# A GNN encoder's edge sort: bucket matrix with two-byte operands, products moved between engines and steps

## The reference

```python
x = emb[x_ids]
def _spmm(row, col, vals, x):
    msg = vals[:, None] * x[col]
    return jax.ops.segment_sum(msg, row, num_segments=N)
def _layer(x_prev, row, col, vals, W_a, b_a, W_b, b_b):
    h = _spmm(row, col, vals, x_prev)
    z = (h + x_prev) @ W_a.T + b_a + h * x_prev @ W_b.T + b_b
    return jnp.where(z >= 0, z, NEG_SLOPE * z)
# x1 = _layer(x, ...); x2 = _layer(x1, ...); x3 = _layer(x2, ...)
return jnp.concatenate((x, x1, x2, x3), axis=1)
```

## Time and profile before

| what | value |
|---|---|
| median of 3 runs | 9519.62 us (9513.02 to 9523.34) |
| time of the profiled execution | 9515.19 us |
| its span | 9513.4 us |
| busy over the span: PE, DVE, ACT, POOL | 92%, 83%, 46%, 60% |
| first reduce of the first pass | 242.8 us |
| last reduce of the second pass | 3179.3 us |

### The profile page before, as it was taken

How to read it: one execution, slowest core, us unless ns; L and a number is a source line. 1 busy time by engine, 2 the same in 40 slices (tenths; PEclk the granted TensorE clock), 3 DMA queues, 4 the chain that set the end, 5 groups by cost and what they waited for, 6 DMA issues and landing times.

```text
span 9513.4 us, 228026 instructions
## 1 busy us (share of the span) xinstructions
PE 8731.2 (92%) x69832; PEld 8032.5 (84%) x69833; DVE 7879.5 (83%) x11265; ACT 4383.1 (46%) x13668; POOL 5665.0 (60%) x3637
## 2 busy tenths in 40 slices
PE   7688886888888589999999999999999999999999
PEld 4577775577777479999999999999999999999999
DVE  7799998899999788877777788877777788877777
ACT  0578775177777346651111366631111566611112
POOL 8688886088888412228888422258888122278885
PEclk8788888888888689999999999999999999999999
DMA  2211111011111887778888677778889577788886
GB/s 80 37 6 6 6 6 19 7 6 6 6 6 6 27 180 280 280 278 284 287 286 286 196 279 281 280 279 287 286 286 286 192 279 282 281 281 286 287 286 205
DMA packets 1005649, 1718.92 MB, mean 181 GB/s; under 512 B 378356, under 2 KB 429624, under 8 KB 1004920
## 3 DMA queue, kind: packets, MB, share of 16 engines
q0 software_dynamic: 378656, 958.17, 33.8%
q1 hardware_dynamic: 499680, 751.43, 21.8%
q10 hardware_dynamic: 127224, 8.24, 3.0%
HBM read 961.68 MB, written 755.66 MB: 181 GB/s over the span
## 4 chain that ended last, share of the span: by engine, by line
PE 66%; DVE 20%; issue 9%; ACT 2%; DMA 1%; ACTq 1%; DVEq 0%; POOL 0%; SPq 0%; POOLq 0%
PE ps L951 34%; PE ps L942 24%; DVE place L1116 7%; DVE hT L1137 4%; DVE hT L1132 4%; PE ps L789 3%; DVE place L1119 2%; ACT work L713 1%; DVE hT L1260 1%; PE ps L839 1%; PE ps L959 1%; PE ps L979 1%; PE ps L980 1%; PE ps L813 1%; DVE place L1121 0%
## 5 line engine op out<-in xcount | busy, mean ns | idle before, releaser
L951 PE MATMUL ps<-work 128*128 128x125 f32 x28416 | 3281.8, 278 | 37.6 <-DVE work L1313 37.6
L951 PEld LDWEIGHTS ps<-work 128*128 128x128 f32 x28416 | 3240.6, 192 | 78.9 <-DVE work L1313 38.8
L547 POOL DMA_INDIRECT work<-messages,work x1776 | 2709.2, 1525 | 621.7 <-issue 621.7
L942 PE MATMUL ps<-xb,work 125*128 x21504 | 2452.2, 276 | 96.1 <-ACT work L713 77.8
L942 PEld LDWEIGHTS ps<-xb,work 125*128 125x128 f32 x21504 | 2421.0, 192 | 127.2 <-issue 127.2
L1313 DVE TENSOR_TENSOR work<-work,iota_p 128x1000 f32<-128x1000 f32 x1776 | 2120.8, 1194 | 35.0 <-ACT work L731 34.4
L713 ACT ACTIVATE work<-ps,work 128x128 f32<-128x128 f32 x5376 | 1537.1, 369 | 1109.5 <-PE ps L942 1109.5
L532 POOL PARTITION_BROADCAST work<-work x672 | 554.5, 827 | 2327.0 <-DMA work<-slot_cols 1283.4
L502 POOL DMA_INDIRECT sorted_edges<-stage,run_idx x798 | 1603.2, 2009 | 475.7 <-ACT stage L644 248.0
L731 ACT ACTIVATE work<-work 128x8 f32<-128x8 f32 x1776 | 534.4, 301 | 2668.3 <-DMA work<-messages,work 2668.3
L839 PEld LDWEIGHTS ps<-hT 128*128 128x128 f32 x12768 | 1621.3, 208 | 115.2 <-issue 90.4
(11 more groups left out here) (206 smaller groups left out, 4522.7 us busy)
## 6 DMA issues: line engine op xcount, KB each, us to landing
messages<-work SPq DMA_DIRECT2D x2688, 256.0 KB, 2.4
work<-messages,work POOLq DMA_INDIRECT x1776, 5.9
out_x<-xb SPq DMA_DIRECT2D x150, 125.0 KB
sorted_edges<-stage,run_idx POOLq DMA_INDIRECT x798, 3.3
work<-slot_cols SPq DMA_DIRECT2D x672, 2.0 KB
work<-lane_places SPq DMA_DIRECT2D x532, 5.2 KB, 2.1
out_x<-xb ACTq DMA_DIRECT2D x4, 1562.5 KB
sorted_edges<-hT SPq DMA_DIRECT2D x4, 908.0 KB
```

The lines of the kernel that those rows point to most:

```text
L547: pool.indirect_dma_start(out=ck[:, n, :, :].rearrange("p h x -> p (h x)"), out_offset=None, in_=flat, in_offset=bass.IndirectOffsetOnAxis ...
L942: last = t.matmul(ps[:, n % PR, j * D:(j + 1) * D], col_hot[:, n % OHR, j * P:(j + 1) * P], x_flat[:, bass.ds(offs[n], D)], start=True, st ...
L951: last = t.matmul(part[n], ck[:, n, j // CH, j % CH * D:(j % CH + 1) * D], sel[:, n % SELB, j, :], start=j == 0, stop=j == CHB - 1)
```

## The change

- `iota_b` is dropped. In its place `iota_bl` holds each bucket number 24 times running, 2400 two-byte values in spare room of `work`. The bucket matrix compares the keys with this written-out operand.
- In VectorE's queue the bucket matrix of w+2 moves ahead of L1119, right behind the reduce of w.
- The product with `packed` moves from the end of window w to the middle of window w+1, behind its part number (`move_packed`). The last window's is done after the loop.
- GpSimd multiplies by `value` only the first 14 lanes (`POOLL`); VectorE does the other 10 in `move_packed`.
- GpSimd's multiply runs two windows ahead of its scatter instead of one.
- `ACTL` rises from 18 to 20; VectorE's part matrix has 4 lanes and now stands ahead of the slot matrix.

```diff
-ACTL = 18
+ACTL = 20
+POOLL = 14
...
-        iota_b = sb("iota_b", [P, NB], BF16)
...
+        IB0 = IR0 + SPARE // 2
+        iota_bl = wb[:, 2 * IB0:2 * IB0 + OHW].rearrange("p (b l) -> p b l", l=LANES)
...
-            count(iota_b[:, :], [[1, NB]])
+            count(iota_bl, [[1, NB], [0, LANES]])
...
             def move_values(p, i, q):
                 n = WOFF[p] + i * 2 + q
                 pool.wait_ge(in_slot_ready, n + 1)
-                g.tensor_tensor(out=moved[q][:, :, 1, :], in0=in_slot,
-                                in1=value[p][:, bass.ds(i * (2 * LANES) + q * LANES, LANES)][:, :, None].to_broadcast([P, LANES, SLOTS]),
+                g.tensor_tensor(out=moved[q][:, 0:POOLL, 1, :], in0=in_slot[:, 0:POOLL, :],
+                                in1=value[p][:, bass.ds(i * (2 * LANES) + q * LANES, POOLL)][:, :, None].to_broadcast([P, POOLL, SLOTS]),
                                 op=ALU.mult).then_inc(valued_ready, 1)
...
                 move_values(p, 0, 0)
                 move_values(p, 0, 1)
-                scatter(p, 0, 0, True)
-                move_values(p, 1, 0)
-                scatter(p, 0, 1, True)
+                for q in range(2):
+                    move_values(p, 1, q)
+                    scatter(p, 0, q, True)
 
                 def both(i, q):
-                    move_values(p, i + q, 1 - q)
+                    move_values(p, i + 1, q)
                     scatter(p, i, q, False)
 
-                pairs(pool, 1, half - 1, both)
+                pairs(pool, 1, half - 2, both)
+                both(half - 1, 0)
+                scatter(p, half - 1, 1, False)
                 scatter(p, half, 0, False)
...
             def one_hot(p, n, q):
                 return v.tensor_tensor(oh[:, q, :].rearrange("p (b l) -> p b l", l=LANES),
                                        key[:, bass.ds(n * LANES, LANES)][:, None, :].to_broadcast([P, NB, LANES]),
-                                       iota_b[:, :, None].to_broadcast([P, NB, LANES]), ALU.is_equal).then_inc(onehot_ready, 1)
+                                       iota_bl, ALU.is_equal).then_inc(onehot_ready, 1)
+
+            def move_packed(p, w, q):
+                n = WOFF[p] + w
+                dve.wait_ge(in_slot_ready, n + 1)
+                v.tensor_tensor(moved[q][:, POOLL:LANES, 1, :], in_slot[:, POOLL:LANES, :],
+                                value[p][:, bass.ds(w * LANES + POOLL, LANES - POOLL)][:, :, None].to_broadcast([P, LANES - POOLL, SLOTS]), ALU.mult)
+                v.tensor_tensor(moved[q][:, :, 0, :], in_slot, packed[p][:, bass.ds(w * LANES, LANES)][:, :, None].to_broadcast([P, LANES, SLOTS]),
+                                ALU.mult).then_inc(moved_ready, 1)
...
                                 ALU.max).then_inc(rank_read, 1)
+                if more:
+                    one_hot(p, w + 2, q)
                 dve.wait_ge(rank_read, n + 1)
...
                 v.tensor_scalar(part_of, raised, ROUND, -ROUND, ALU.add, ALU.add).then_inc(part_found, 1)
+                if not (first and q == 0):
+                    move_packed(p, w - 1, 1 - q)
                 dve.wait_ge(part_found, n + 1)
                 v.scalar_tensor_tensor(slot, part_of, -float(SLOTS), at, ALU.mult, ALU.add).then_inc(slot_link, 1)
-                if more:
-                    one_hot(p, w + 2, q)
                 if not first:
                     dve.wait_ge(ordered, n - 1)
+                v.tensor_tensor(to_part[q][:, ACTL:LANES, :], part_of[:, ACTL:LANES][:, :, None].to_broadcast([P, LANES - ACTL, P]),
+                                iota_p[:, None, :].to_broadcast([P, LANES - ACTL, P]), ALU.is_equal)
                 dve.wait_ge(slot_link, n + 1)
...
-                v.tensor_tensor(to_part[q][:, ACTL:LANES, :], part_of[:, ACTL:LANES][:, :, None].to_broadcast([P, LANES - ACTL, P]),
-                                iota_p[:, None, :].to_broadcast([P, LANES - ACTL, P]), ALU.is_equal)
-                dve.wait_ge(in_slot_ready, n + 1)
-                v.tensor_tensor(moved[q][:, :, 0, :], in_slot, packed[p][:, bass.ds(w * LANES, LANES)][:, :, None].to_broadcast([P, LANES, SLOTS]),
-                                ALU.mult).then_inc(moved_ready, 1)
...
                 window(p, half, 0, False, False)
+                move_packed(p, 2 * half, 0)
```

More of the change, by code:

```diff
@@ L196, in graph_layers @@
         iota_run = wb[0:NBD, 2 * IR0:2 * IR0 + SPARE]
-        assert IR0 + SPARE <= 20560
+        IB0 = IR0 + SPARE // 2
+        iota_bl = wb[:, 2 * IB0:2 * IB0 + OHW].rearrange("p (b l) -> p b l", l=LANES)
+        assert IB0 + OHW // 2 <= 20560
         hot = [hb[:, r * LT:(r + 1) * LT] for r in range(HR)]
```

## The result

The changed kernel takes 9179.43 us (median of 4 runs, 9172.53 to 9193.25) against 9521.48 for the kernel before (4 runs): a ratio of 0.9644, 95% interval 0.9631 to 0.9656. Its profiled execution took 9172.53 us, 342.7 less than the one of before. The direction and the new bound were as forecast, the size was not: 9232 was forecast, with 9190 as the low end.

A forecast was written before the change was run, and what follows sets the result against it. VectorE, at times standing behind GpSimd, set the 9.80 us step; ScalarE would then bind at 8.65. 253 x (9.80 - 8.65) = 290 us saved, plus 2 for edges: 9227 profiled, 9232 median; 8-in-10 range 9190 to 9360.

The forecast's parts named there:

- The mechanism: Window loop of the two sorts: ScalarE replaces VectorE as the bound, 8.65 us a step against VectorE's 8.11; chance 62%.
- ScalarE doesn't bind: Rival, window loop: ScalarE's two added lanes cost less than read; step 8.4 us, 354 us saved, 9168; chance 5%.
- The signs: Window loop, if right: even steps of 8.6 to 8.8 us, reduce released by L658 with about 0.5 us idle.
- GpSimd stays late: Rival, window loop: GpSimd's late multiply still meets VectorE; 9.05 us a step, 190 us saved, 9332; chance 18%.
- the deferral: Packed product moved into the next step: cost nil, since TensorE's ordering still ends about 3 us ahead of the stage copy.
- the sum of ScalarE: ScalarE's work per window: 7.75 us plus 0.84 for two more lanes, 8.59 to 8.77, taken as 8.65.
- The bucket matrix: L1105 on VectorE: writing out the re-read operand halves its stream, 2.66 us to 1.41.
- VectorE's sum: VectorE's operations in a window, start to start: 8.11 us against 9.23, or 9.36 if the bucket matrix stays whole.
- its issue of 3.40 us: A disturbed GpSimd DMA issue (1.57 us undisturbed), ending 0.18 after L1132; set against the skill's inference that issues aren't stalled.
- The edges: Outside the steady loop: 2 us added for the written-out operand's iota at the start; first windows unchanged.

The follow-up runs named there:

- the second profile: The changed kernel run and profiled again with nothing altered: 9198.76 us, ratio 0.9648 to the kernel before.

## Why the prediction missed, point by point

**The mechanism held.** ScalarE became the bound, the reduce was released by L662, GpSimd's multiply went under the reduce, the clock rose. By its number the 8.43 lies in the range of the rival "ScalarE doesn't bind" (8.11 to 8.5), but ScalarE did bind. The signs were met in part: the reduce waits 0.26 to 0.40 us for a forecast of 0.5, and the steps are not even. The rival "GpSimd stays late" did not happen here, but it was the nearest danger: taking back the matrix, the deferral or the ten lanes, one at a time, brings it about (with the matrix for 0.18 us only; the rest is VectorE's own sum).

**The step that failed is the sum of ScalarE.** It was put at 8.59 to 8.77 us and taken at 8.65; it measured 8.43. Term by term: two lanes of copy 0.57 for 0.60, the pass 0.21 for 0.24, the stage copy 0.13 for 0.23, because the next copy starts 0.13 after that one's start, and 0.06 allowed for a gap that is not there. Together 0.22 us, times 253 steps 56 us, which is the whole miss: 9227 forecast for the profiled execution, 9172.5 measured. The trace of before had the number whole, in the one place where ScalarE had a backlog (the first of these rows stands in the earlier trace rows, the other two are not shown ahead):

```profile
335.12 5.36 ACT L655 ACTIVATE hT<-iota_p,place 128x128 f32<-128x128 f32 x18 [43.78 <-issue]
...
342.64 0.23 ACT L644 ACTIVATE stage<-ps 128x96 f32<-128x96 f32 x1
342.77 5.35 ACT L655 ACTIVATE hT<-iota_p,place 128x128 f32<-128x128 f32 x18
```

From 335.12 to 342.77 is 7.65 us for 18 lanes, start to start. With the two lanes as measured (0.78) that gives 8.43. The prediction built 7.75 and up to 7.93 from durations in a step that had idle time. The range then broke on the same term: its low end stands for a step of 8.5, just under ScalarE's lowest sum of 8.58, and only 5% went to a cheaper ScalarE.

**The bucket matrix** was taken at 1.41 and is 1.40. A whole 2.66 would have cost 1.03 us a step (9.46). The Trainium skill (Vector Engine (DVE) Microarchitecture Reference, section 5.1) had two elements a cycle for this form; the row of L1109 agrees.

**VectorE's sum** was 8.11 and is 8.03: the steps of 8.03 occur wherever VectorE catches up after a delay.

**GpSimd.** The multiply was taken at 1.3 and is 1.31. Its step was put at 8.1 at least. In the changed kernel it idles 0.71 us before the multiply. What the prediction left out is how firmly its place in the step is tied to VectorE: an issue that starts under a two-input operation ended 1.44 to 1.46 us after it, and the multiply behind it can hold the next such operation. With one lane less on ScalarE this made steps of 8.34, only 0.1 below the new step. The prediction also named nowhere the wait of one window's scatter for the landing of the last one's, which is small in the trace of before (8.2 us in all); in the variants it is there in most steps, and no run shows that it costs anything.

**The deferral** was costed at nil, by ScalarE's cover of the ordering. That was right for its own price, and wrong for its worth: the run without it is 1.05 us a step slower. It separates VectorE's products from GpSimd's multiply. The prediction never asked what the operations of the two engines would meet without it.

The skill (SBUF — State Buffer, Who interferes with whom) says that a VectorE operation with two SBUF inputs and a GpSimd operation that reads SBUF exclude each other. The 2.47 and 2.98 us agree. Its inference that issues of DMAs are not stalled by such operations is not borne out: 3.00 us for an issue under the long bucket matrix, 1.57 to 1.58 for one under the reduce. The prediction set its issue of 3.40 us beside the end of L1132. The operation it belongs to is the one before that, as the end of this row shows (1547.67; the issue ended 1.45 us later, at 1549.12):

```profile
1545.01 2.66 DVE L1105 TENSOR_TENSOR work<-work,iota_b 128x2400 bf16<-128x2400 bf16 x1
```

**The edges** were put at +2 us and came out at +2.5, by luck. The written-out operand's iota took 2.63 us for the 2 taken, and the first reduce began 0.7 us later (243.5 for 242.8). The eighth began 20.4 us earlier. Of that some 13 us is the end of the gathers, which moved back in the second profile; the rest lies in the two steps behind the pause. The end was 22.8 us later, and there the cause is not settled. In the first layer the aggregation and dense part took 1178 to 1179 us in both profiles of before and with the written-out operand alone, and 1183 to 1187 in the changed kernel and every variant that reorders GpSimd's and VectorE's queues. Over the three layers that is 3534 and 3536 us before and 3555 in both profiles of the changed kernel, so most of the 22.8. GpSimd's idle time ahead of its gathers in the layers reads so, before and after (busy, mean ns, idle):

```profile
L547 POOL DMA_INDIRECT work<-messages,work x1776 | 2709.2, 1525 | 621.7 <-issue 621.7
```
```profile
L551 POOL DMA_INDIRECT work<-messages,work x1776 | 2712.7, 1527 | 636.4 <-issue 631.7
```

The code there is the same, only its place in the queue's instructions differs. That this matters is a guess; no run tested it.

**What each part is worth,** as steps: all 8.43; without the matrix 9.46, without the deferral 9.48, without the ten lanes 9.04; the matrix alone 9.11; none 9.80. The three removals cost 1.03, 1.05 and 0.61, twice the whole gain of 1.37. They are not terms of a sum: each alone lets two engines run into each other again. Three edits were never taken back by themselves: the bucket matrix's place right behind the reduce, the part matrix's ahead of the slot matrix, and GpSimd's multiply two windows ahead of its scatter. What each is worth is not known.

## What to carry to other kernels

Read an engine's cost per step from start to start, at a place where it has a backlog, rather than adding durations: neighbours overlap, and 0.2 us in 253 steps was the whole error. Where VectorE and GpSimd both read SBUF, place is worth as much as length: put GpSimd's operation under one that doesn't exclude it, and ask of every moved operation what it no longer meets. Before giving an engine relief, ask what else ends just below the present step, and look for it in the lengths of the operations and not in the idle time alone: 0.18 us in a matrix's record were the next limit. A wait that shows in a profile (for landed DMAs, here) is no bound while what follows it ends at the same time however long the wait was. And keep long runs of DMA issues off an engine that a loop waits for (43 us here).

## What was not expected of the hardware

- Four DMA issues of x to the output held ScalarE's queue for 43.0 to 43.8 us, and the whole sort with it; behind the first sort they took as long (13.26 and 29.92 us for two each), but there no loop waited for ScalarE.
- In 15 of 253 steps of the changed kernel a step was over 9.3 us (11 of them 9.7): the ordering needed 7.20 to 7.22 us for 5.59 (8.85 once), and the part matrix waited 0.9 to 1.2 us for it (2.8 once). The mean granted clock of 0.99 hides the cause. Just after the start of each of these 15 orderings, and nowhere else in the two stretches, the granted clock fell to the lower of its two levels, 0.50, as in this stretch (last three figures: granted clock, DMA share, GB/s):

```profile
515.26 7.20 PE L843 MATMUL ps<-hT 128*128 128x96 f32 x48 [0.63 <-ACT stage L648]
515.50:518.90 3.40, 3.40 (x18) 3.40 (x18) 3.40 (x2) 3.40 (x13) 2.93 (x3) 0.50 0.16 7
```

  TensorE had done what it does in every step, with 0.6 us of idle time before the ordering as in the others; why the clock fell there stays open. The second profile has 16 such falls, and 16 long steps with them. The next three or four steps were mostly 8.03, so ScalarE's pace, and the total, hardly suffered.
